# RMS attention: rotation by shuffles, softmax sums by 32-block transposes, and scores as 64-row products over rows stacked by SBUF-to-SBUF transfers

## What is computed

```python
q = _rmsnorm(x @ Wq); k = _rmsnorm(x @ Wk); v = x @ Wv      # norm over all heads of a token
q = q.reshape(b, t, K, G, H)                                # K = 4 key heads, G = 4, H = 16
q = q * qcos + _rotate_half(q) * qsin                       # the same for k
q = q * rsqrt(H)
logits = einsum('btkgh,bskh->bkgts', q, k)
probs = softmax(logits); enc = einsum('bkgts,bskh->btkgh', probs, v)
return enc.reshape(b, t, N * H) @ Wout
```

## Time and profile before

| | |
|---|---|
| runs shown | 1579.04, 1576.71, 1581.8 us; median 1579.04 |
| profiled execution | 1580.17 us, span 1578.4 us |
| PE, DVE, ACT, POOL busy | 92%, 62%, 48%, 36% of the span |
| this stage | some 1324 to 1476 us of the span |
| first scores, scores of the last unit, last projection | 1365.0, 1452.3, 1473.7 us |

### The profile page before, as it was taken

One profiled execution on the slowest core, in us unless ns is written; L12 is line 12 of the kernel. 1 busy time (PEld: TensorE's weight loads), 2 busy tenths in 40 slices (PEclk: granted clock), 3 DMA queues, 4 the chain that ended last, 5 costly groups with the idle time before them and its releaser, 6 DMA issues. The chain is left out here.

```text
span 1578.4 us, 29465 instructions
## 1 busy us (share of the span) xinstructions
PE 1459.4 (92%) x10783; PEld 1125.6 (71%) x10810; DVE 978.5 (62%) x2186; ACT 754.7 (48%) x1876; POOL 561.0 (36%) x556
## 2 busy tenths in 40 slices
PE   6999999999899899999999989998998898999897
PEld 4778777787689677777777757985555696633586
DVE  5766667665674766566565657567674754376763
ACT  5565655746235334343433434543454462577352
POOL 2835528363137165435142103532000371100074
PEclk9999999999999999999999999999999999999998
DMA  4122221222363434203031009234000633000434
GB/s 148 60 81 78 89 91 54 71 67 85 135 257 98 164 94 136 72 18 123 0 102 39 1 0 380 73 108 175 2 1 1 222 104 119 1 1 1 185 96 140
DMA packets 54285, 144.89 MB, mean 92 GB/s; under 512 B 9104, under 2 KB 23824, under 8 KB 54032
## 3 DMA queue, kind: packets, MB, share of 16 engines
q1 hardware_dynamic: 36496, 84.99, 15.3%
q0 software_dynamic: 17664, 58.21, 10.9%
HBM read 104.90 MB, written 38.27 MB: 91 GB/s over the span
## 5 line engine op out<-in xcount | busy, mean ns | idle before, releaser
L145 POOL TENSOR_SCALAR ln_var<-ln_moments 128x4 f32<-128x4 f32 x16 | 3.9, 245 | 415.4 <-DVE ln_moments L130 263.2
L412 POOL DMA_INDIRECT expert_rows<-s_y,s_to_row x92 | 91.0, 989 | 58.0 <-ACT s_y L736 37.0
L1370 ACT ACTIVATE s_scratch<-s_bank,s_neg_max 128x128 f32<-128x128 f32 (+3 forms) x128 | 67.2, 528 | 88.2 <-DVE s_neg_max L1460 88.0
L1460 DVE TENSOR_REDUCE s_neg_max<-s_bank 128x1 f32<-128x128 f32 (+3 forms) x128 | 59.4, 486 | 55.1 <-PE s_bank L1260 55.0
L2769 POOL TENSOR_TENSOR s_w_hi<-s_w_raw,zero 128x1024 fp32r<-128x1024 f32 x25 | 55.3, 2214 | 100.4 <-PE s_memory L81 77.1
L1258 PE MATMUL s_bank<-s_k,s_q 128*128 128x128 f32 (+3 forms) x256 | 88.7, 442 | 1.5 <-DVE s_v L1455 0.8
L2454 ACT ACTIVATE s_exps<-s_bank,s_rms 128x512 f32<-128x512 f32 x128 | 76.6, 695 | 20.0 <-PE s_bank L2334 20.0
L953 DVE TENSOR_TENSOR s_h_e<-s_bank,s_silu_e 128x176 f32<-128x176 f32 x92 | 31.4, 341 | 83.6 <-ACT s_silu_e L724 79.7
L79 PE MATMUL s_bank<-xn_t_hi,s_w_hi 128*128 128x512 f32 x192 | 80.3, 418 | 1.3 <-DVE xn_t_lo L212 1.2
L405 POOL DMA_INDIRECT s_xg<-normed_rows,s_from_row x64 | 63.4, 991 | 38.5 <-DVE s_from_row L848 20.2
L1277 PE MATMUL s_bank<-s_probs_t,s_v 128*128 128x512 f32 (+3 forms) x256 | 74.7, 435 | 2.3 <-ACT s_probs_t L1378 2.3
(11 more groups left out here) (426 smaller groups left out, 4915.1 us busy)
## 6 DMA issues: line engine op xcount, KB each, us to landing
s_expert_w_lo<-experts_lo SPq DMA_DIRECT2D x32, 608.0 KB, 13.2
s_e_lo<-in_experts POOLq DMA_DIRECT2D x32, 304.0 KB, 3.1
experts_hi<-s_e_hi POOLq DMA_DIRECT2D x32, 304.0 KB, 2.5
experts_lo<-s_e_lo POOLq DMA_DIRECT2D x32, 304.0 KB, 2.9
s_expert_w_hi<-experts_hi SPq DMA_DIRECT2D x16, 608.0 KB, 12.2
s_w_raw<-in_wa_o SPq DMA_DIRECT2D x16, 512.0 KB, 3.6
s_yg<-expert_rows SPq DMA_DIRECT2D x32, 256.0 KB, 4.7
s_raw<-in_shared SPq DMA_DIRECT2D x16, 384.0 KB, 5.9
```

Source lines behind the costliest of these rows:

```text
L412: pool.indirect_dma_start(out=y_rows[:, :], out_offset=bass.IndirectOffsetOnAxis(ap=to_row[:, i:i + 1].bitcast(U32), axis=0), in_=y[:, i % ...
L1370: act.activation(probs[:, h % 2, r, 0:(r + 1) * P], score_bank(h, r), ACT.Exp, bias=neg_max[:, 4 * h + r:4 * h + r + 1], accum_out=row_sum ...
L1460: dve.tensor_reduce(neg_max[:, 4 * h + r:4 * h + r + 1], score_bank(h, r), AX.X, ALU.max, negate=True).then_inc(max_done, 1)
```

## The change

It replaces the half-turn product by a DVE shuffle of partitions inside each 32-slot (the sign goes into the sin table); the product that spreads the sums by a DVE transpose of 32x32 blocks, a reciprocal of 16 columns, and a second such transpose that spreads the inverse; the second copy of o by a second PSUM bank. It stacks `k_hi` and `k_lo` of a head in 64 rows and `q_both` twice in 64 rows, by transfers from SBUF to SBUF on SP (eight of 32 partitions x 512 columns, 64 KB each, for a unit's q, eight for a batch's k); the scores of a head are then one product. On DVE, `invert(G-1)` and `divide(G-1)` come ahead of `rotate` and `split_q` of G+1. `project_out(G-1)` comes at j = 3 of unit G. `spread_rms(1)` goes from j = 0 to j = 1 of unit 0, without the fillers ahead of it, and `apply_rms(1)` behind the first `split_q` of the loop; the fillers of the tail go from 23 to 16.

```diff
-        acc, s_bank, o_bank, sum_bank = banks[:2], banks[2:6], banks[6], banks[7]
+        acc, s_bank, o_banks, sum_bank = banks[:2], banks[2:6], banks[6:8], banks[7]
...
+        k_rows, q_rows = sb("k_rows", [P, 2, TOK], F32R), sb("q_rows", [P, 2, 2, S], F32R)
...
+            def stack_q(G):
+
+                sp.wait_ge(q_split, G + 1)
+                if G:
+                    sp.wait_ge(q_stacked, STACK * G)
+                if G >= 2:
+                    sp.wait_ge(scores_ready, 16 * (G - 1))
+                for g in range(KV_HEADS):
+                    for i in range(2):
+                        sp.dma_start(f32(q_rows[slot(2 * (g % 2) + i), G % 2, g // 2, :]),
+                                     f32(q_both[slot(g), G % 2, :])).then_inc(q_stacked, 16)
+
+            stack_k(0)
+            stack_q(0)
+            stack_k(1)
+            for G in range(1, UNITS):
+                stack_q(G)
...
                 if j == 0:
-                    pe.wait_ge(q_split, G + 1)
-                    pe.wait_ge(k_lo_done, b + 1)
+                    pe.wait_ge(q_stacked, STACK * (G + 1))
+                    pe.wait_ge(k_stacked, STACK * (b + 1))
                 keys = slice(b * S + j * P, b * S + (j + 1) * P)
-                for part in (k_hi, k_lo):
-                    for g in (2 * h, 2 * h + 1):
-                        last = pe.matmul(s_bank[g][:], part[slot(g), keys], q_both[slot(g), G % 2, :],
-                                         start=part is k_hi, stop=part is k_lo, skip_group_check=True)
...
+                for i in range(2):
+                    pe.matmul(s_bank[2 * h + i][:], k_rows[two_slots(i), h, keys], q_rows[two_slots(i), G % 2, h, :],
+                              start=True, stop=True, skip_group_check=True).then_inc(scores_ready, 1)
...
-                    if G == 0 and j == 0:
+                    if G == 0 and j == 1:
                         pe.wait_ge(sums_read, 2)
-                        keep_busy(pe, res, sum_bank[:], 9)
                         spread_rms(1, sum_bank)
...
-                    if G >= 2 and j == 1:
-                        project_out(G - 2)
-                    if G and j == 2:
-                        finish(G - 1)
+                    if G and j == 3:
+                        project_out(G - 1)
...
-            keep_busy(pe, res, s_bank[0][:], 23)
+            keep_busy(pe, res, s_bank[0][:], 16)
             project_out(UNITS - 1)
...
+                dve.stream_shuffle(half_turned[:], now, turn_rows).then_inc(turn_done, 1)
+                dve.wait_ge(turn_done, n + 1)
                 dve.tensor_tensor(now, now, to_cos, ALU.mult).then_inc(cos_part, 1)
+                dve.tensor_tensor(turned_part[:], half_turned[:], to_sin, ALU.mult).then_inc(sin_part, 1)
...
+            def invert(G):
+                o_bank = o_banks[G % 2]
                 dve.wait_ge(o_ready, TB * (G + 1))
...
+                dve.transpose(by_query[:], o_bank[:]).then_inc(sums_turned, 1)
...
+                dve.reciprocal(by_query_inverse[:], by_query[:].rearrange("p (b r) -> p b r", r=SLOT)[:, :, HD]).then_inc(sums_inverted, 1)
...
+                dve.transpose(inverse[:], by_query_inverse[:].unsqueeze(2).broadcast_to([P, S // SLOT, SLOT])).then_inc(inverse_done, 1)
...
             for G in range(UNITS):
                 if G:
-                    copy_o(G - 1)
+                    invert(G - 1)
+                    divide(G - 1)
                 if G + 1 < UNITS:
-                    rotate(*divmod(G + 1, PER_KV), sum_bank)
+                    rotate(*divmod(G + 1, PER_KV))
                     split_q(G + 1)
-                if G:
-                    divide(G - 1)
+                if G == 0:
+                    apply_rms(1, sum_bank)
```

More of the change, by code:

```diff
@@ L2168, in rms_gqa_stage @@
             sem("v_ready"), sem("v_done"), sem("sums_read"), sem("rms_step"), sem("rms_done"))
-        rms_spread, rms_applied, half_turned, half_read, cos_part, rotated = (
-            sem("rms_spread"), sem("rms_applied"), sem("half_turned"), sem("half_read"), sem("cos_part"), sem("rotated"))
+        rms_spread, rms_applied, turn_done, sin_part, cos_part, rotated = (
+            sem("rms_spread"), sem("rms_applied"), sem("turn_done"), sem("sin_part"), sem("cos_part"), sem("rotated"))
         k_hi_done, k_lo_done, q_hi_done, q_split = sem("k_hi_done"), sem("k_lo_done"), sem("q_hi_done"), sem("q_split")
-        scores_ready, exp_done, o_ready, o_copied, sum_spread, inverse_done, o_done = (
-            sem("scores_ready"), sem("exp_done"), sem("o_ready"), sem("o_copied"), sem("sum_spread"),
+        k_stacked, q_stacked = sem("k_stacked"), sem("q_stacked")
+        scores_ready, exp_done, o_ready, sums_turned, sums_inverted, inverse_done, o_done = (
+            sem("scores_ready"), sem("exp_done"), sem("o_ready"), sem("sums_turned"), sem("sums_inverted"),
             sem("inverse_done"), sem("o_done"))
@@ L2181, in rms_gqa_stage @@
         slot = lambda g: slice(g * SLOT, (g + 1) * SLOT)
+        two_slots = lambda i: slice(2 * i * SLOT, 2 * (i + 1) * SLOT)
+        STACK = 16 * 2 * KV_HEADS
         def ring(m):
@@ L2197, in _, with stack_k @@
             sp.dma_start(w_raw[:], t["wd_q"].rearrange("c p n -> p c n")).then_inc(w_loaded, 16)
-            for to, src in ((half_turn, "half_turn"), (cos, "cos"), (sin, "sin"), (sum_sel, "sum_sel"), (low_rows, "low_rows")):
+            for to, src in ((cos, "cos"), (sin, "sin"), (low_rows, "low_rows")):
                 sp.dma_start(to[:], t[src]).then_inc(loaded, 16)
             sp.dma_start(bv[:], t["v_ones"].partition_broadcast(P)).then_inc(loaded, 16)
+            def stack_k(b):
+                sp.wait_ge(k_lo_done, b + 1)
+                for g in range(KV_HEADS):
+                    for i, part in enumerate((k_hi, k_lo)):
+                        sp.dma_start(f32(k_rows[slot(2 * (g % 2) + i), g // 2, batch(b)]),
+                                     f32(part[slot(g), batch(b)])).then_inc(k_stacked, 16)
+            def stack_q(G):
[4 more added lines that the diff above has]
+                    sp.wait_ge(scores_ready, 16 * (G - 1))
+                for g in range(KV_HEADS):
+                    for i in range(2):
[6 more added lines that the diff above has]
+                stack_q(G)
         @block.gpsimd
@@ L2288, in spread_rms @@
                 last.then_inc(rms_spread, 1)
[L2290 to L2295, removed]
             pe.wait_ge(ones_made, 1)
@@ L2343, in attend @@
                 if j == 0:
-                    if G:
-                        pe.wait_ge(o_copied, G)
+                    if G >= 2:
+                        pe.wait_ge(o_done, G - 1)
+                    elif G:
+                        pe.wait_ge(rms_applied, 2)
                     else:
-                        pe.wait_ge(half_read, 3)
                         pe.wait_ge(v_done, 2 * B)
                 for g in range(KV_HEADS):
-                    last = pe.matmul(o_bank[slot(g), :], v[:, b * TB + j, slot(g)], exps[:, s % 2, g, :],
+                    last = pe.matmul(o_banks[G % 2][slot(g), :], v[:, b * TB + j, slot(g)], exps[:, s % 2, g, :],
                                      start=j == 0, stop=j == TB - 1, skip_group_check=True)
                 last.then_inc(o_ready, 1)
[L2354 to L2360, removed]
             def project_out(G):
@@ L2494, in apply_rms, with rotate @@
                 dve.tensor_tensor(scaled[:, b, 1, :], bank[:], sin[:], ALU.mult).then_inc(rms_applied, 1)
-            def rotate(b, f, bank):
+            turn_rows = [SLOT // 2 * (i // HD) + (i + HD // 2) % HD for i in range(SLOT)]
+            def rotate(b, f):
                 n = turn_of(b, f)
@@ L2501, in rotate @@
                     dve.wait_ge(rms_applied, b + 1)
-                dve.wait_ge(half_turned, n + 1)
+                dve.wait_ge(fill_squared, fills.index((b, f)) + 1)
                 dve.wait_ge(rotated, n)
-                dve.tensor_tensor(turned_part[:], bank[:], to_sin, ALU.mult).then_inc(half_read, 1)
+                dve.stream_shuffle(half_turned[:], now, turn_rows).then_inc(turn_done, 1)
+                dve.wait_ge(turn_done, n + 1)
                 dve.tensor_tensor(now, now, to_cos, ALU.mult).then_inc(cos_part, 1)
-                dve.wait_ge(half_read, n + 1)
+                dve.tensor_tensor(turned_part[:], half_turned[:], to_sin, ALU.mult).then_inc(sin_part, 1)
+                dve.wait_ge(sin_part, n + 1)
                 dve.wait_ge(cos_part, n + 1)
@@ L2582, in _ @@
                     measure(0, 2)
-            copy_o(UNITS - 1)
+            invert(UNITS - 1)
             divide(UNITS - 1)
@@ L3524, in layout @@
     t["cos"], t["sin"] = (by_both(np.concatenate([f(sinusoid)] * 2, 1).astype(np.float32)) for f in (np.cos, np.sin))
[L3526 to L3530, removed]
+    t["sin"] *= np.tile(np.where(np.arange(HD) < HD // 2, -1, 1), P // HD).astype(np.float32)[:, None]
```

(2 more changed lines are left out.)

55 lines of the change are left out of this document (18 added, 37 removed).

## The result

Before: median 1580.42 us of four runs (1576.71 to 1583.31). After: 1604.86 of four (1601.61 to 1609.64). The ratio is 1.0151, interval 1.0127 to 1.0176: slower by 24.4 us. The sign was forecast; the size was not: 1590 was forecast, 10.7 us above before, and 1604.86 lies above the range's end of 1603.

A forecast was written before the change was run, and what follows sets the result against it. RMS attention was taken as bound by ACT with PE's extra products in its way; after, 10.3 + 15.3 + 5 x 15.9 + 17.1 = 122.2 us against 108.7, +13.5, with the head +10.7: 1590 us, range 1575 to 1603.

The forecast's parts named there:

- a new wait: RMS attention: each unit's scores wait for q through PE, DVE and SP; 14.6 us a unit, 15.9 with fallen clock.
- DVE's term: Step (b) of the unit's chain: transposes, reciprocal, division, shuffle, rotation and split on DVE, 7.67 us.
- The clock falls in each of the long gaps: PE's idle gaps in units: half clock adds 0.3 us for scores and 1.0 for `attend`.
- The tail: From unit 7's first scores to the last projection: 17.1 us, against 21.4 before.
- step (c): SP's part of the unit's chain: seven issues at 0.475, a 1.8 us landing and 0.2 for hand-overs, 5.3 us.
- the head: Stage before unit 0: half-turn products leave PE's prologue, q's first transfers land about 0.4 us late; -2.8 us.
- the rival of dear issues: SP's transfers at 0.64 us an issue: six units grow 1.2 each, head 1; 1598 us. Dearer pieces together: chance 0.20.
- The rival built on it: SP hands over eight transfers in a burst: 11.2 us a unit, 1562 us; chance 0.15 together with cheap pieces.
- unit 0: First unit of the stage: table load, three blocks, first pair and moved spread, 10.3 us.
- half-turns: Three half-turn products leave PE's dense prologue in the head, at most 1.06 us each: -3.2 us.
- Scores and `attend` at the low clock: Step (a) of the unit's chain: 0.45 plus 1.13 us, growing by 0.3 and 1.0 at half clock.
- the rival that the scores don't shrink: PE's 64-row score products run one after another, 0.70 us stays: 0.25 us a unit; no chance given.

The follow-up runs named there:

- the six-issue kernel: The changed kernel with six transfers for a unit's q in place of eight, the two middle slots of each product in one: 1595.82 us, ratio 1.0111.
- with the clock kept: Rotation and split ahead of inversion and division, plus six fillers before unit 0's first scores, nine behind block 0, and a semaphore per k batch: 1566.04 us, ratio 0.9905.
- the split-first kernel: The changed kernel with rotation and split of unit G+1 put back ahead of inversion and division of G-1 on DVE: 1567.07 us, ratio 0.9912.
- with six issues: Split first with unit 0's fillers, plus six q transfers a unit and the projection in two halves behind blocks 2 and 3: 1564.69 us, ratio 0.9900.
- the kernel with fillers: The changed kernel with 20 products of zeros on PE behind the projection of units 1 to 6: 1602.16 us, ratio 1.0118.

## Why the prediction was right, and where it was wrong

*Right.* The sign and its cause: a new wait, closed over PE, DVE and SP, sets the unit, and ACT stands idle inside it. Splitting first opens the chain and turns the loss into a gain. DVE's term was 7.67 us and measured 7.64: the transposes and the shuffle cost 0.71 to 0.75, little more than the copy of that size, 0.68; the single pieces are off by up to 0.07 both ways, which the sum hides. (For the shuffle the estimate from the price in the Trainium skill, VectorE: DVE Perf Modes, "Rules for kernel authors", was 0.6 us; the trace has 0.72 to 0.75.) The clock falls in each of the long gaps, and that costs 1.39 us a unit; 1.3 was forecast. The tail came out at 17.5 for 17.1.

*Wrong: the price of an issue, step (c).* The prediction said: "Those go to scattered rows, the new ones are plain 32x512 blocks, so I take 0.475." Measured was 0.62, near the end named beside it. Seven of them make 1.0 us more; with a landing of 2.0 for 1.8, and hand-overs of 0.09 for 0.2, (c) was 6.45 us for 5.3. In units 1 to 6 this is 6.8 us, and in the head it makes q's first transfers 1.5 us late for 0.4: 7.9 of the 13.8 us (24.5 - 10.7) that were missing. It was the rival of dear issues that came true, together with the fallen clock; the forecast had two bounds whose sources differ in kind, HBM and SBUF, and took the wrong one. It chose by the target of the transfer, but issues from SBUF into scattered rows and into plain blocks cost nearly the same, 0.64 and 0.62.

The rule of the Trainium skill that was weighed (DMA: Bandwidth & Descriptors, "Issuing engines are not separate DMA queues"), that starting transfers is usually little beside moving them, does not hold for eight in a row: 4.36 us for seven issues, which follow one another, against 2.0 for the landing of the last. The rival built on it, 1562 us, is ruled out by the six-issue kernel, where every issue left out shortens the unit; that 1565 to 1567 was reached by moving the split is another mechanism.

*Wrong: unit 0.* 13.8 us for 10.3. The late transfers and the first exponentials' table left PE idle for 1.50 and 2.21 us at the unit's start, the nine fillers that stood there before were gone, and the clock was 0.50 for the next products (the spread took 2.08 us for 1.16); 12.3 with the clock kept shows 1.5 us of it (1.2 beside the split-first kernel). The prediction counted the fall in the steady units and not here. Another 0.95 is the wait for unit 1's transfers, which shows once the clock is kept and is gone with six issues (11.35). What is left, 1 us, holds a gap of ACT of 0.85 ahead of block 2, against the 0.3 that was put down; what would close it wasn't tried.

*Small terms.* The half-turns left the head 2.3 us shorter, not 3.2. Scores and `attend` at the low clock took 1.15 and 2.00 us, 3.15 for 2.9, in each of five units. Most of that is the scores: at full clock, in the kernel with fillers, four products of 64 rows hold PE for 0.66 us (1411.63 to 1412.29), where 0.45 was put down and eight of 32 rows took 0.70. So the rival that the scores don't shrink came nearly true, at the small price that it was given. And one of the four gaps behind the earlier trace rows, called two to three microseconds long, is 3.50; nothing hangs on it.

The sum: 7.9 for transfers, 3.5 for unit 0, 0.9 for half-turns, 5 x 0.27 = 1.4 for scores and `attend`, 0.4 for the tail, less 6 x 0.03 = 0.2 for DVE: 13.9 against 13.8.

## What to carry to other kernels

Where a producer's transfers feed the next step of a loop, follow the loop once round over every queue before looking at any cost: here one exchange in DVE's list is worth 38 us, while the prices that the forecast missed came to 14. Take the price of a transfer's issue from a row with the same kind of source, and count issues, not bytes. Where a new wait is put ahead of PE's work, price what comes behind it at the lower clock as well, also at the one place where the loop starts.

## Not expected of the hardware

An issue on SP takes 0.42 us from HBM and 0.59 to 0.61 from SBUF, whether 32 or 128 partitions move. A 32x32 block transpose of 128x512 f32 on DVE, read from PSUM or spread from 16 columns, costs 0.71 to 0.72 us, about as much as a plain pass (0.69), and loading the shuffle's mask 0.01, where 0.13 had been allowed. And one DVE operation beside a POOL pass of 128x1024 took 2.72 us instead of 0.75, in unit 0 of the kernel after. It lies off the path there, but with unit 0's clock kept it stands ahead of the transfers that unit 1 waits for. DVE's timeline:

```profile
1369.07 2.72 DVE L2517 SCALAR_TENSOR_TENSOR s_q_both<-s_q_hi,s_low_rows,s_qk 128x512 fp32r<-128x512 f32 x1
```

POOL's:

```profile
1368.63 2.61 POOL L2255 TENSOR_TENSOR s_w_lo<-s_w_raw,s_w_hi 128x1024 fp32r<-128x1024 f32 x1
```

In the kernel after and in all eight kernels made from it the two coincide, and this operation takes 2.72 or 2.73 us; in the kernel before the same split starts at 1375.05, behind POOL's pass (1368.24 to 1370.60), and takes 0.75. That the one slows the other is likely from this, but no run moved only one of them.
